# Moving a power and its followers by two steps on GpSimd, and joining eight group sums into five, in a fused graph network kernel

## The chip, the cores and the metric

The kernel runs on one core of one Trainium2 chip. The metric is the device time of one execution in microseconds (us). Names of the engines in the profile: PE is TensorE (PEld its weight loads), DVE is VectorE, ACT is ScalarE, POOL is GpSimd, SP is SyncE, which here only issues DMAs.

## The reference

64 graphs with 128 nodes and 128 features, and a dense weighted adjacency each. A first part (five small graph convolutions over subsets of the first 25 nodes) is added to x and normalised; a second part (five layers of aggregation and a gated recurrent cell over all 128 nodes) is added to that and normalised again.

```python
GROUPS = [list(range(25)), list(range(9)), [0, 9, 10, 11, 12, 13, 14],
          [6, 7, 8, 12, 13, 14], [3, 4, 5, 9, 10, 11]]
def graph_conv(x, adj, W, b):
    A = adj + eye(n)
    deg = sum(A, -1)
    dinv = where(deg == 0, 0, deg ** -0.5)
    return relu((dinv[:, :, None] * A * dinv[:, None, :]) @ (x @ W) + b)
fused = 0
for g, idx in enumerate(GROUPS):
    h = graph_conv(x[:, idx], adj[:, idx][:, :, idx], W1[g], b1[g])
    fused[:, idx] += softmax(fusion_w)[g] * graph_conv(h, ..., W2[g], b2[g])
x = layernorm(x + fused)
h = x
for l in range(5):
    agg = (adj != 0)^T @ (h @ weight[l])
    r, z = sigmoid(...), sigmoid(...)      # of agg and h
    n = tanh(i_n + r * h_n)
    h = (1 - z) * n + z * h
x = layernorm(x + h * mask)
```

## The kernel before

**Work and steps.** The 64 graphs are 4 chunks of 16 (CHUNKS), a chunk is 4 visits of 4 graphs (SB). The recurrent part goes through 80 windows, here called steps: for each chunk 5 layers times 4 visits, so 20 steps make a round, numbered `w.i` from 0 to 19. Neighbouring steps are of different visits, so that the engines can overlap them. A step is, on TensorE, nine 512-column multiplications with the state's high and low part (lines 1063 to 1065 through `product`), transposes of an older state (`turn`, line 1050), nine multiplications with the aggregated neighbours, and the aggregation of a coming step (line 1057). On ScalarE it is the two sigmoids and the tanh (`ng`, line 622) and copies out of PSUM; on VectorE `cg` (884, 887), the end of the step before (`dg` times `zg`, 796, and the new state `hT`, 798), and the low parts `hlo` (784) and `glo` (790); on GpSimd the difference `dg = hT - ng` (434), which waits for the tanh.

**The first part rides along.** While chunk c is in its round, the first part of chunk c + 1 is spread over the steps of that round, at step numbers written out by hand in `Plan`. Each engine's program is one list in order, with semaphores between the engines; nothing is reordered at run time, so what stands ahead in an engine's list delays what is behind. For the place that concerns us, at step 7 and 8 TensorE and ScalarE make the results of the second convolution: `fused` (16 graphs in 32 columns each, group 0) and `part` (groups 1 to 4, line 514). At step 9 (GATHER) GpSimd adds the groups of `part` into `fused`. At step 10 (BACK) TensorE transposes `fused` back (line 1003, waiting for all ADDS sums), and VectorE adds that to `xn` (753) in steps 10, 12 and 13. From step 11 on VectorE takes the statistics (760, 764) and GpSimd turns them into `rs` and `nm` (394 to 399, with a power), with which ScalarE normalises (524).

**Two chunks ahead.** In rounds 0 and 1 the adjacency of chunk c + 2 is prepared as well: VectorE sums the degrees at step 8 (669 to 679), GpSimd raises them to the power -0.5 (337) behind the `dg` of step 8, VectorE multiplies the adjacency with them at the end of step 9 (`scaled`, 685 and 689), and GpSimd spreads the rows into block diagonal tiles (346, six instructions with 358) behind the `dg` of step 10. TensorE needs those at step 2 of the next round. Rounds 2 and 3 have none of this, and round 3 no next chunk at all.

**Opening.** The first part of chunk 0 runs ahead of the steps; there the sums of the groups are VectorE's (743), and GpSimd has the powers of chunks 0 and 1.

**The sums.** Groups 1 to 4 are lists of nodes; `runs` cuts a list into runs of neighbouring node numbers, 8 over the five tiles of groups 1 to 4 (72, 72, 16, 96 and four times 48 elements in each partition). Each sum waits for the one before it.

Of the kernel before, what the change touches and what calls it, by code (L numbers as in the profile page):

```python
# [5 lines left out]
GROUPS = [list(range(25)), [0, 1, 2, 3, 4, 5, 6, 7, 8], [0, 9, 10, 11, 12, 13, 14],  # L6
          [6, 7, 8, 12, 13, 14], [3, 4, 5, 9, 10, 11]]
NG = len(GROUPS)
FN = 25
NP = 32  # L10
# [7 lines left out]
CB = 16  # L18
CHUNKS = B // CB
# [7 lines left out]
TILES = [(0, 4, b) for b in range(0, CB, 4)] + [(1, 8, 0), (1, 8, 8)] + [(g, 16, 0) for g in (2, 3, 4)]  # L27
# [3 lines left out]
TB = [t for t in range(NT) if TILES[t][0] != 0]  # L31
OFF = {}
# [8 lines left out]
def runs(nodes):  # L41

    out = []
    for i, v in enumerate(nodes):
        if out and v == out[-1][1] + out[-1][2]:
            out[-1][2] += 1
        else:
            out.append([i, v, 1])
    return [tuple(r) for r in out]
# [29 lines left out]
class Plan:  # L79

    ADJ, Y, HA, HB, SA, SB, OA, OB, GATHER, BACK, REST = 2, 3, 4, 5, 6, 7, 7, 8, 9, 10, (12, 13)
    DEGREES, SCALED, SPREAD = 8, 9, 10
    ONES = {2: 0, 5: 1, 11: 2, 13: 3}
    STATS1 = {11: 0, 14: 1, 15: 2, 16: 3}
    APPLY1 = {12: [(0, 0)], 13: [(0, 1)], 15: [(1, 0)], 16: [(1, 1), (2, 0)], 17: [(2, 1), (3, 0)], 18: [(3, 1)]}
# [8 lines left out]
def next_chunk(w):  # L94

    return w.sg + 1 if w.sg + 1 < CHUNKS else None


def stats1(w):
    c = next_chunk(w)  # L100
    return None if c is None or w.i not in Plan.STATS1 else c * SLOTS + Plan.STATS1[w.i]
# [7 lines left out]
def stats2(w):  # L109
    return None if w.sg == 0 or w.i not in Plan.STATS2 else (w.sg - 1) * SLOTS + Plan.STATS2[w.i]  # L110
# [9 lines left out]
def build(nc, x, adj, nodemask, W1, b1, W2, b2, fusion_w, weight, w_ih, w_hh, b_ih, b_hh, out):  # L120
    f32, f32r = mybir.dt.float32, mybir.dt.float32r
    ALU, ACT, AX = mybir.AluOpType, mybir.ActivationFunctionType, mybir.AxisListType
    ctx = ExitStack()
    with ctx:
        ctx.enter_context(nc.allow_non_contiguous_dma(reason="small rows of the adjacency"))

        def sb(name, shape, dt=f32):
            return ctx.enter_context(nc.sbuf_tensor(name, shape, dt))
# [53 lines left out]
        fused = sb("fused", [128, CB * NP])  # L182
        part = sb("part", [128, COLS_B])
# [24 lines left out]
        def b1c(g, c):  # L208
# [22 lines left out]
        gathered, dev1, dev2, ln1_dve, ln1_pool, hT_ok = map(sem, (  # L231
            "gathered", "dev1", "dev2", "ln1_dve", "ln1_pool", "hT_ok"))
# [25 lines left out]
        def group_cols(g):  # L258

            mine = [t for t in TB if TILES[t][0] == g]  # L260
            return OFF[mine[0]], OFF[mine[-1]] + ROWS[mine[-1]]

        def n_runs(tiles):

            return sum(len(runs(GROUPS[TILES[t][0]])) for t in tiles)
        ADDS = n_runs(TB)
        SP_ADJ, ACT_ADJ, POOL_ADJ = TB[0:2] + TB[3:4] + TA[0:1], TB[2:3] + TB[4:5] + TA[1:2], TA[2:4]
        XT_SP, XT_POOL = range(0, NT - 2), range(NT - 2, NT)

        def gather_part(t, i, v, n):  # L270

            g, k, b0 = TILES[t]
            into = fused[:].rearrange("p (b n) -> p b n", n=NP)[:, b0:b0 + k, v:v + n]
            return into, part[:, OFF[t] + i * k:OFF[t] + (i + n) * k].rearrange("p (n k) -> p k n", k=k)

        @block.sync
        def _(sp):
# [43 lines left out]
        def _(pool):  # L321
# [12 lines left out]
            def power(c):  # L334

                pool.wait_ge(deg_ok, c + 1)
                nc.gpsimd.tensor_tensor(dinv[:, c, :], deg[:], minus_half[:], ALU.pow).then_inc(pow_ok, 1)
# [25 lines left out]
            def ones(visit):  # L363

                pool.wait_ge(xa_in, 64 * (visit // SLOTS) + 64)
                ab = an[:, visit * SB:(visit + 1) * SB, :]
                nc.gpsimd.tensor_scalar(ab, ab, 0.0, 0.0, ALU.is_equal, ALU.is_equal).then_inc(a_ok, 1)

            def gather(c):

                n_add = 0
                pool.wait_ge(oa_ok, c + 1)
                for t in TB:
                    g, k, b0 = TILES[t]
                    pool.wait_ge(ob_ok, (NG - 1) * c + g)
                    for i, v, n in runs(GROUPS[g]):
                        if n_add:
                            pool.wait_ge(gathered, ADDS * c + n_add)
                        n_add += 1
                        into, these = gather_part(t, i, v, n)  # L380
                        nc.gpsimd.tensor_tensor(into, into, these, ALU.add).then_inc(gathered, 1)  # L381

            def norm1(visit):

# [16 lines left out]
            def deviation1(visit):  # L401

                pool.wait_ge(ln1_st, visit + 1)
                o = visit % SLOTS
                deviation(ag1[:, o], rs1[:, o], nm1[:, o], dev1, visit).then_inc(ln1_rs, 1)

            def deviation2(visit):

                pool.wait_ge(ln2_st, visit + 1)
                o = visit % SLOTS  # L410
                deviation(ag2[:, o], rs2[:, o], nm2[:, o], dev2, visit).then_inc(ln2_rs, 1)
# [17 lines left out]
            for w in ALL_WINDOWS:  # L429
                c = next_chunk(w)  # L430
                if c is not None and w.i == Plan.GATHER:
                    gather(c)
                pool.wait_ge(n_ok, w.k + 1)
                nc.gpsimd.tensor_tensor(dg[:, w.k % 2, :], hT[:, w.slot, :], ng[:, w.k % 2, :], ALU.subtract).then_inc(d_ok, 1)  # L434
                if stats1(w) is not None:
                    deviation1(stats1(w))
                if stats2(w) is not None:
                    deviation2(stats2(w))
                if c is not None and w.i in Plan.ONES:
                    ones(c * SLOTS + Plan.ONES[w.i])  # L440
                if w.sg + 2 < CHUNKS and w.i == Plan.DEGREES:
                    power(w.sg + 2)
                if w.sg + 2 < CHUNKS and w.i == Plan.SPREAD:
                    spread(w.sg + 2)
# [193 lines left out]
        def _(dve):  # L638
            link = counter(dve, dve_c)
            TT, TS, STT = nc.vector.tensor_tensor, nc.vector.tensor_scalar, nc.vector.scalar_tensor_tensor  # L640
# [4 lines left out]
            for t, (g, k, _) in enumerate(TILES):  # L645
                for i, v, n in runs(GROUPS[g]):
                    nc.vector.memset(member[:, t, v:v + n], 1.0)
                    nc.vector.reduce_sum(unit[:, t, v:v + n],
                                         ident[:, i * k:(i + n) * k].rearrange("p (n k) -> p n k", k=k), AX.X)
# [80 lines left out]

            def gather(c):

                n_add = 0
                dve.wait_ge(oa_ok, c + 1)
                for t in TB:
                    g, k, b0 = TILES[t]
                    dve.wait_ge(ob_ok, (NG - 1) * c + g)
                    for i, v, n in runs(GROUPS[g]):
                        if n_add:
                            dve.wait_ge(gathered, ADDS * c + n_add)  # L740
                        n_add += 1
                        into, these = gather_part(t, i, v, n)
                        TT(into, into, these, ALU.add).then_inc(gathered, 1)

            def add(c, first, some=range(PACK)):

# [108 lines left out]
            for w in ALL_WINDOWS:  # L855
                k, s, p = w.k, w.slot, w.k % 2
                c = next_chunk(w)
# [50 lines left out]
        def _(pe):  # L908
# [90 lines left out]
            def back(c):  # L999

                pe.wait_ge(gathered, ADDS * (c + 1))
                for t in range(CB // PACK):
# [189 lines left out]
```

## Time and profile before

| what | value |
|---|---|
| median of 3 runs | 559.54 us (559.19 to 559.57) |
| profiled execution | 555.05 us |
| its span, first to last instruction | 553.0 us |
| TensorE busy | 521.4 us, 94% |
| VectorE busy | 436.0 us, 79% |
| ScalarE busy | 369.4 us, 67% |
| GpSimd busy | 253.0 us, 46% |
| mean granted clock of TensorE | 0.983 of full |

A busy share is an average over the opening (the first 50 us), the rounds and the closing. The chain of work that ended last goes through TensorE for 67% of the span, VectorE for 11% and GpSimd for 8%. Starts of rows count from the start of the span. Ends of matrix multiplications are modelled, since they overlap each other; the distance from start to start tells the pace.

### The profile page before, as it was taken

Reading aid. Unit: us, or ns where it says so; the run is one execution under the profiler, and the core shown is the slowest. Engines: PE = TensorE matmul, PEld = TensorE weight load, DVE = VectorE, ACT = ScalarE, POOL = GpSimd, SP = SyncE. Lnnn points to the kernel's source line nnn. Section 1 sums busy time; section 2 is a strip of 40 time slices with the busy share of each in tenths; the row PEclk is TensorE's granted clock in tenths of the full one; section 3 lists DMA queues with packets and bytes.
Section 4 is the critical chain, followed back from the end, with each engine's and each line's share of the span. In section 5 each row is a group of like instructions: output and inputs, shape, how many; then the busy total and the mean of one; then the engine's idle time right before and its main releaser. Section 6 shows DMA issues by size and latency. Waiting matters only on the chain.

```text
span 553.0 us, 8593 instructions
## 1 busy us (share of the span) xinstructions
PE 521.4 (94%) x3021; PEld 446.0 (81%) x3021; DVE 436.0 (79%) x970; ACT 369.4 (67%) x682; POOL 253.0 (46%) x304
## 2 busy tenths in 40 slices
PE   8886999989999999989999999999999999999980
PEld 7775888868888889868888888888888888888860
DVE  4276765779988986879988986779988998878785
ACT  2434765656785766777787667677887678886644
POOL 7167333267543245376552344364552335432335
PEclk9898999999999999999999999999999999999995
DMA  4966610000000000000000000000000000010002
GB/s 103 247 177 162 159 33 3 1 0 1 2 1 1 0 28 25 21 20 21 0 2 1 0 1 21 20 20 20 0 1 1 2 1 20 22 36 0 2 1 76
DMA packets 35666, 17.30 MB, mean 31 GB/s; under 512 B 4429, under 2 KB 35584, under 8 KB 35624
## 3 DMA queue, kind: packets, MB, share of 16 engines
q1 hardware_dynamic: 32569, 15.13, 10.4%
q10 hardware_dynamic: 2639, 1.42, 0.9%
q8 instruction: 25, 0.41, 0.3%
q0 software_dynamic: 416, 0.20, 0.2%
q14 instruction: 17, 0.14, 0.1%
HBM read 12.54 MB, written 4.19 MB: 30 GB/s over the span
## 4 chain that ended last, share of the span: by engine, by line
PE 67%; DVE 11%; POOL 8%; ACT 5%; issue 4%; SPq 2%; DMA 1%; DVEq 0%; POOLq 0%; ACTq 0%
PE p L1065 15%; PE p L1063 15%; PE p L1064 14%; PE p L1057 9%; PE p L1050 6%; POOL dg L434 3%; PE p L958 3%; POOL fused L381 2%; DVE cg L884 2%; DVE cg L887 2%; PE p L932 2%; POOL rs L397 1%; DVE xn L753 1%; PE p L951 1%; PE p L941 1%
## 5 line engine op out<-in xcount | busy, mean ns | idle before, releaser
L434 POOL TENSOR_TENSOR dg<-hT,ng 128x512 f32<-128x512 f32 x80 | 124.9, 1561 | 262.4 <-ACT ng L622 262.4
L1063 PE MATMUL p<-hhi,wh 128*128 128x512 f32 x240 | 101.1, 421 | 0.6 <-DVE hlo L784 0.6
L1063 PE MATMUL p<-ghi,wf 128*128 128x512 f32 x240 | 101.7, 424 | 0.0
L1065 PE MATMUL p<-ghi,wf 128*128 128x512 f32 x240 | 94.8, 395 | 0.0
L1065 PE MATMUL p<-hhi,wh 128*128 128x512 f32 x240 | 94.3, 393 | 0.0
L1064 PE MATMUL p<-glo,wf 128*128 128x512 f32 x240 | 94.1, 392 | 0.0
L1064 PE MATMUL p<-hlo,wh 128*128 128x512 f32 x240 | 93.7, 390 | 0.0
L884 DVE SCALAR_TENSOR_TENSOR cg<-p,biasc,rg 128x512 f32<-128x512 f32 x80 | 59.9, 748 | 41.1 <-ACT rg L609 40.4
L609 ACT ACTIVATE rg<-p,gb 128x512 f32<-128x512 f32 x80 | 55.4, 692 | 36.5 <-PE p L1065 31.0
L622 ACT ACTIVATE ng<-cg,biasc 128x512 f32<-128x512 f32 x80 | 57.9, 723 | 24.0 <-DVE cg L887 23.8
L1057 PEld LDWEIGHTS p<-an,nat 128*128 128x128 f32 x512 | 66.9, 191 | 5.2
L620 ACT ACTIVATE zg<-p,gb 128x512 f32<-128x512 f32 x80 | 55.0, 688 | 19.5 <-PE p L1065 19.5
L1057 PE MATMUL p<-an,nat 128*128 128x128 f32 x512 | 67.4, 275 | 0.0
L784 DVE TENSOR_TENSOR hlo<-hT,hhi 128x512 fp32r<-128x512 f32 x76 | 66.5, 876 | 0.9
L887 DVE TENSOR_TENSOR cg<-cg,p 128x512 f32<-128x512 f32 x80 | 55.0, 688 | 8.7 <-DVE cg L884 0.5
L790 DVE TENSOR_TENSOR glo<-p,ghi 128x512 fp32r<-128x512 f32 x80 | 55.2, 690 | 7.6 <-ACT ghi L578 7.6
L798 DVE TENSOR_TENSOR hT<-ng,dg 128x512 f32<-128x512 f32 x80 | 55.5, 694 | 2.8
L607 ACT COPY nat<-p 128x512 f32<-128x512 f32 x64 | 37.8, 591 | 27.1 <-PE p L1050 26.5
L796 DVE TENSOR_TENSOR dg<-zg,dg 128x512 f32<-128x512 f32 x80 | 55.5, 694 | 0.0
L1050 PE MATMUL p<-ident,hT 128*128 128x128 f32 x320 | 49.0, 276 | 6.9 <-DVE hT L798 6.6
L1065 PEld LDWEIGHTS p<-ghi,wf 128*128 128x128 f32 x240 | 45.3, 189 | 10.5
L1065 PEld LDWEIGHTS p<-hhi,wh 128*128 128x128 f32 x240 | 45.0, 188 | 10.0
(131 smaller groups left out, 853.1 us busy)
## 6 DMA issues: line engine op xcount, KB each, us to landing
xn<-in_x_dram SPq DMA_DIRECT2D x8, 512.0 KB, 4.8
an<-in_adj_dram SPq DMA_DIRECT2D x8, 512.0 KB, 7.1
out_dram<-xn SPq DMA_DIRECT2D x16, 256.0 KB, 2.3
xt<-in_x_dram SPq DMA_DIRECT2D x16, 50.0 KB
w<-in_L_gnn_W_dram ACTq DMA_DIRECT2D x1, 640.0 KB, 6.9
w<-in_L_gnn_W_dram SPq DMA_DIRECT2D x1, 640.0 KB, 7.9
zg<-in_L_gnn_weight_dram ACTq DMA_DIRECT2D x1, 320.0 KB, 7.9
xt<-in_x_dram SPq DMA_DIRECT2D x8, 36.0 KB
```

The lines of the kernel that those rows point to most:

```text
L434: nc.gpsimd.tensor_tensor(dg[:, w.k % 2, :], hT[:, w.slot, :], ng[:, w.k % 2, :], ALU.subtract).then_inc(d_ok, 1)
L622: nc.scalar.activation(ng[:, p, :], cg[:, p, :], ACT.Tanh, bias=bin_).then_inc(n_ok, 1)
L784: TT(hlo[:, m % SLOTS, :], hT[:, m % SLOTS, :] if source is None else source[:], hhi[:, m % SLOTS, :], ALU.subtract).then_inc(lo_ok, 1)
L796: TT(dg[:, p, :], zg[:, p, :], dg[:, p, :], ALU.mult).then_inc(e_ok, 1)
L798: TT(hT[:, s, :], ng[:, p, :], dg[:, p, :], ALU.add).then_inc(h_ok, 1)
L884: STT(cg[:, p, :], PH[:], bhn, rg[:, p, :], ALU.add, ALU.mult).then_inc(t1_ok, 1)
L887: TT(cg[:, p, :], cg[:, p, :], PI[:], ALU.add).then_inc(c_ok, 1)
L1050: last = TR(bank[:, q * 128:(q + 1) * 128], src(q), ident[:])
L1057: last = MM(bank[:, q * N:(q + 1) * N], src(q), an[:, b + q, :], start=True, stop=True)
L1063: MM(bank[:], w[:, 0, cols], xhi, start=start, stop=False)
L1064: MM(bank[:], w[:, 0, cols], xlo, start=False, stop=False)
L1065: return MM(bank[:], w[:, 1, cols], xhi, start=False, stop=stop)
```

## The change

GpSimd's power of the degrees is moved from step 8 to step 10 (still behind `dg`), VectorE's scaling from the end of step 9 to the end of step 11, GpSimd's spreading from step 10 to step 12. VectorE's summing of the degrees stays in step 8. The eight sums of the groups become five, on GpSimd in the rounds and on VectorE in the opening: one for both tiles of group 1 (144 elements), two for group 2 (96 and 16), one each for groups 3 and 4 (96), whose two runs of three nodes lie six apart and are put into one access pattern. A sum waits for an earlier one only where both write the same nodes.

```diff
--- before.py
+++ after.py
@@ -79,7 +79,7 @@
 class Plan:
 
     ADJ, Y, HA, HB, SA, SB, OA, OB, GATHER, BACK, REST = 2, 3, 4, 5, 6, 7, 7, 8, 9, 10, (12, 13)
-    DEGREES, SCALED, SPREAD = 8, 9, 10
+    DEGREES, POWER, SCALED, SPREAD = 8, 10, 11, 12
     ONES = {2: 0, 5: 1, 11: 2, 13: 3}
     STATS1 = {11: 0, 14: 1, 15: 2, 16: 3}
     APPLY1 = {12: [(0, 0)], 13: [(0, 1)], 15: [(1, 0)], 16: [(1, 1), (2, 0)], 17: [(2, 1), (3, 0)], 18: [(3, 1)]}
@@ -263,15 +263,25 @@
         def n_runs(tiles):
 
             return sum(len(runs(GROUPS[TILES[t][0]])) for t in tiles)
-        ADDS = n_runs(TB)
         SP_ADJ, ACT_ADJ, POOL_ADJ = TB[0:2] + TB[3:4] + TA[0:1], TB[2:3] + TB[4:5] + TA[1:2], TA[2:4]
         XT_SP, XT_POOL = range(0, NT - 2), range(NT - 2, NT)
 
-        def gather_part(t, i, v, n):
-
-            g, k, b0 = TILES[t]
-            into = fused[:].rearrange("p (b n) -> p b n", n=NP)[:, b0:b0 + k, v:v + n]
-            return into, part[:, OFF[t] + i * k:OFF[t] + (i + n) * k].rearrange("p (n k) -> p k n", k=k)
+        def gather_parts():
+
+            rows_ = fused[:].rearrange("p (b n) -> p b n", n=NP)
+
+            def cols(g):
+                a, b = group_cols(g)
+                return part[:, a:b]
+            yield 1, 0, (rows_[:, :, 0:9].rearrange("p (t k) n -> p t k n", t=2),
+                         cols(1).rearrange("p (t n k) -> p t k n", t=2, n=9))
+            yield 2, 0, (rows_[:, :, 9:15], cols(2)[:, CB:].rearrange("p (n k) -> p k n", k=CB))
+            yield 2, 1, (rows_[:, :, 0:1], cols(2)[:, 0:CB].rearrange("p (n k) -> p k n", k=CB))
+            for g in (3, 4):
+                v = GROUPS[g][0]
+                yield g, 2, (rows_[:, :, v:v + 12].rearrange("p k (s n) -> p s n k", s=2)[:, :, 0:3, :],
+                             cols(g).rearrange("p (s n k) -> p s n k", s=2, n=3))
+        ADDS = 5
 
         @block.sync
         def _(sp):
@@ -368,17 +378,12 @@
 
             def gather(c):
 
-                n_add = 0
                 pool.wait_ge(oa_ok, c + 1)
-                for t in TB:
-                    g, k, b0 = TILES[t]
+                for g, done, (into, these) in gather_parts():
                     pool.wait_ge(ob_ok, (NG - 1) * c + g)
-                    for i, v, n in runs(GROUPS[g]):
-                        if n_add:
-                            pool.wait_ge(gathered, ADDS * c + n_add)
-                        n_add += 1
-                        into, these = gather_part(t, i, v, n)
-                        nc.gpsimd.tensor_tensor(into, into, these, ALU.add).then_inc(gathered, 1)
+                    if done:
+                        pool.wait_ge(gathered, ADDS * c + done)
+                    nc.gpsimd.tensor_tensor(into, into, these, ALU.add).then_inc(gathered, 1)
 
             def norm1(visit):
 
@@ -438,7 +443,7 @@
                     deviation2(stats2(w))
                 if c is not None and w.i in Plan.ONES:
                     ones(c * SLOTS + Plan.ONES[w.i])
-                if w.sg + 2 < CHUNKS and w.i == Plan.DEGREES:
+                if w.sg + 2 < CHUNKS and w.i == Plan.POWER:
                     power(w.sg + 2)
                 if w.sg + 2 < CHUNKS and w.i == Plan.SPREAD:
                     spread(w.sg + 2)
@@ -730,17 +735,12 @@
 
             def gather(c):
 
-                n_add = 0
                 dve.wait_ge(oa_ok, c + 1)
-                for t in TB:
-                    g, k, b0 = TILES[t]
+                for g, done, (into, these) in gather_parts():
                     dve.wait_ge(ob_ok, (NG - 1) * c + g)
-                    for i, v, n in runs(GROUPS[g]):
-                        if n_add:
-                            dve.wait_ge(gathered, ADDS * c + n_add)
-                        n_add += 1
-                        into, these = gather_part(t, i, v, n)
-                        TT(into, into, these, ALU.add).then_inc(gathered, 1)
+                    if done:
+                        dve.wait_ge(gathered, ADDS * c + done)
+                    TT(into, into, these, ALU.add).then_inc(gathered, 1)
 
             def add(c, first, some=range(PACK)):
 
```

## Rows read from the trace of the kernel before

**Rows 1.** Busy times of the engines on the page: us, share of the span, instructions.

```profile
PE 521.4 (94%) x3021; PEld 446.0 (81%) x3021; DVE 436.0 (79%) x970; ACT 369.4 (67%) x682; POOL 253.0 (46%) x304
```

**Rows 2.** Timeline of TensorE: start, duration, instruction, [idle before].

```profile
119.17 0.39 PE L1064 MATMUL p<-hlo,wh 128*128 128x512 f32 x1
119.40 0.39 PE L1065 MATMUL p<-hhi,wh 128*128 128x512 f32 x1
121.79 0.66 PE L1003 MATMUL p<-ident,fused 128*128 128x128 f32 x4 [2.00 <-POOL fused L381]
...
138.89 0.60 PE L1050 MATMUL p<-ident,hT 128*128 128x128 f32 x4
...
248.16 0.65 PE L1003 MATMUL p<-ident,fused 128*128 128x128 f32 x4 [2.05 <-POOL fused L381]
...
371.99 0.39 PE L1065 MATMUL p<-hhi,wh 128*128 128x512 f32 x1
372.45 0.66 PE L1003 MATMUL p<-ident,fused 128*128 128x128 f32 x4
```

**Rows 3.** Timeline of GpSimd (POOL), steps 8 to 13 of round 0.

```profile
115.18 2.28 POOL L337 TENSOR_TENSOR dinv<-deg,minus_half 128x9 f32<-128x9 f32 x1
117.42 4.32 POOL L381 TENSOR_TENSOR fused<-fused,part 128x72 f32<-128x72 f32 x8
...
128.40 0.84 POOL L346 TENSOR_TENSOR bda<-am,ksel 100x400 f32<-100x400 f32 x1
129.21 1.98 POOL L358 TENSOR_TENSOR bdb<-am,ksel 72x144 f32<-72x144 f32 x5
132.19 1.64 POOL L434 TENSOR_TENSOR dg<-hT,ng 128x512 f32<-128x512 f32 x1 [1.00 <-ACT ng L622]
133.92 1.08 POOL L394 TENSOR_SCALAR rs<-ag 128x4 f32<-128x4 f32 x1
...
138.74 1.29 POOL L434 TENSOR_TENSOR dg<-hT,ng 128x512 f32<-128x512 f32 x1 [0.29 <-ACT ng L622]
144.03 1.63 POOL L434 TENSOR_TENSOR dg<-hT,ng 128x512 f32<-128x512 f32 x1 [4.00 <-ACT ng L622]
```

**Rows 4.** Chain that ended last, sums of round 2: start, duration, what.

```profile
367.80 0.81 POOL fused L381
```

**Rows 5.** Timelines of the opening, of TensorE, VectorE (DVE) and GpSimd.

```profile
30.84 3.42 PE L913 MATMUL p<-ng,cg 128*128 128x384 f32 x10
34.62 0.66 PE L1003 MATMUL p<-ident,fused 128*128 128x128 f32 x4 [0.36 <-DVE fused L743]
...
31.61 2.95 DVE L743 TENSOR_TENSOR fused<-fused,part 128x72 f32<-128x72 f32 x8 [0.37 <-ACT part L514]
...
31.24 1.84 POOL L337 TENSOR_TENSOR dinv<-deg,minus_half 128x9 f32<-128x9 f32 x1 [0.96 <-DVE deg L678]
```

**Rows 6.** Timeline of VectorE, steps 9 to 13 of round 0.

```profile
119.87 0.40 DVE L689 TENSOR_TENSOR am<-am,dinv 128x225 f32<-128x225 f32 x1
...
129.02 0.77 DVE L784 TENSOR_TENSOR hlo<-hT,hhi 128x512 fp32r<-128x512 f32 x1
...
135.31 0.75 DVE L884 SCALAR_TENSOR_TENSOR cg<-p,biasc,rg 128x512 f32<-128x512 f32 x1 [0.37 <-ACT rg L609]
...
137.70 0.69 DVE L798 TENSOR_TENSOR hT<-ng,dg 128x512 f32<-128x512 f32 x1
139.15 0.69 DVE L790 TENSOR_TENSOR glo<-p,ghi 128x512 fp32r<-128x512 f32 x1 [0.76 <-ACT ghi L578]
...
140.94 0.67 DVE L784 TENSOR_TENSOR hlo<-hT,hhi 128x512 fp32r<-128x512 f32 x1
```

**Rows 7.** Timelines of GpSimd and VectorE beside a power, step 14 of round 0.

```profile
151.37 1.04 POOL L397 TENSOR_TENSOR rs<-rs,minus_half 128x4 f32<-128x4 f32 x1
...
151.43 0.67 DVE L784 TENSOR_TENSOR hlo<-hT,hhi 128x512 fp32r<-128x512 f32 x1
```

**Rows 8.** Timeline of ScalarE (ACT), step 12 of round 0.

```profile
136.58 0.89 ACT L524 ACTIVATE xn<-xn,nm,rs 128x128 f32<-128x128 f32 x2 [1.30 <-POOL nm L399]
```

## Prediction

> **What bounds the kernel now.** I read four things in this order. First the page's busy line: TensorE is busy 94% of the span, so outside the opening and the closing every pause of TensorE should count in full [rows 1]. Second, TensorE's own timeline, looking for the places where it pauses. Its 512-column multiplications normally start 0.23 us apart (119.17, 119.40). In step 9 to 10 of a round that rhythm breaks ahead of the four transposes of line 1003, which turn the group sums back. In the first round (round 0) the last multiplication starts at 119.40, so the transposes could start at 119.63, and they start at 121.79: a pause of 2.16 us. The row of 121.79 itself gives 2.00, counted from the modelled end, and that of the second round 2.05, so the second pause is 2.16 + 0.05 = 2.21 us. In the third (round 2) the start is due at 371.99 + 0.23 = 372.22 and comes at 372.45: only 0.23 us [rows 2]. Third, GpSimd's timeline at that place, to see what is late. In the first round GpSimd does the power of the degrees (2.28 us), then eight sums in 4.32 us, and they end at 121.74, which releases the transposes [rows 3]. The third round has no chunk two ahead of it, so it has no power there; its eight sums start right behind dg. That round is an experiment that the kernel already holds: without the power the pause is 0.23 us. Fourth, VectorE: behind the transposes it adds the result to x and goes on with a chain that has hardly a pause for several steps, so a later start of the transposes is not won back.
>
> **Part 1, the power leaves the path.** In rounds 0 and 1 (the only ones with a chunk two ahead) the power stood at the end of step 8, directly ahead of the sums. With it gone the sums start at 115.2 instead of 117.42. Even at their old length of 4.32 us they would end at 119.5 to 119.8: what is left is the 0.23 us of round 2. So this part alone gives 2.16 - 0.23 = 1.93 and 2.21 - 0.23 = 1.98 us, together 3.9 us.
>
> **Part 2, five sums for eight.** The number of elements is the same (448 per partition); three instructions go, and most waits of one on the one before. The eight old ones take 4.32 us, 0.54 each with the gaps [rows 3]; the dearest, 72 elements with VectorE in the way, is 0.81 [rows 4]. No row shows 144 elements, nor these two patterns over four dimensions. From below: five at 0.54 are 2.7 us; from above: five at the dearest 0.81 are 4.05 us. I take 3.1, nearer the lower end, since the time goes with the instructions more than with the elements, but the average one is now larger. TensorE's room is 119.63 - 115.2 = 4.4 us, so even the upper bound meets it, and TensorE itself then sets the start. That removes the last 0.23 us in each of the three rounds: 0.7 us. The rest of the shortening is hidden behind TensorE's step 10.
>
> **Part 3, the sums of chunk 0 on VectorE.** They take 2.95 us from 31.61 to 34.56. TensorE is at its weight products from 30.84 to 34.26 and starts the transposes at 34.62 [rows 5]. However short the sums become, the transposes can't start before 34.26: the gain is at most 0.36 us and I take 0.35. They wait for the same four group results of ScalarE as the old ones, whose last group began its sums before 34.3 too; for the new ones to be late, five would have to take 2.65 of the 2.95 us that eight took. What follows (addition to x, statistics, the deviation on GpSimd, normalising on ScalarE) is a chain that keeps its length.
>
> Sum of the gains: 2.16 + 2.21 + 0.23 + 0.35 = 4.95, say 5.0 us.
>
> **Part 4, where the power goes.** In step 10 it now stands behind dg, at 128.4, where the spreading was. The spreading took 0.84 + 1.98 = 2.8 us there, and dg of step 11 came at 132.19 after a pause of 1.00 us [rows 3]. The power takes 2.3 us, so dg of step 11 is not late and the pause merely grows. Cost nothing for GpSimd. It is covered by ScalarE's tanh, for which dg waits; without that cover it would be 2.3 us a round.
>
> What it does to VectorE: VectorE's hlo at 129.02 falls in it [rows 6]. Some VectorE operations with both inputs in SBUF do stand still beside GpSimd. A power does not seem to do that: at 151.37 GpSimd starts a power of 1.04 us, and hlo starts at 151.43 and takes 0.67 us, its usual time [rows 7]; in the opening the eight sums on VectorE begin during the power of 31.24 to 33.08 [rows 5]. I take nothing. The Trainium skill says otherwise ("SBUF — State Buffer", § on the shared port pair): a VectorE operation with two SBUF inputs and a GpSimd operation that reads SBUF exclude each other for the whole instruction. By that rule hlo would wait for the end of the power, which is a rival below; by the rows the sum stays as it is.
>
> **Part 5, where the scaling goes.** Its larger instruction is that of 119.87 with 0.40 us; the smaller, on 9 elements, stands ahead of it and I put it and the gap at a third of the whole, so 0.6 us together. They cost nothing in step 9, since VectorE waited behind them for the late transposes [rows 6]. Now they stand at the end of step 11, at about 133.2. VectorE has a pause of 0.37 us at 135.31, so 0.2 us is left, or up to 0.8 if the first of them waits for dg of step 11, which runs until 133.83 (132.19 + 1.64). VectorE meets ScalarE again at 139.15, after a pause of 0.76 us, and that takes up nearly all. But hT of 137.70 ends at 138.39, and TensorE reads it at 138.89 with 0.5 us to spare [rows 2, 6]: 0 to 0.3 us reach TensorE. There is a second way to it: the deviation behind dg. Its first instruction took 1.08 us at 133.92, plainly held by VectorE, and ScalarE stood 1.30 us for its result at 136.58 [rows 3, 8]. With VectorE 0.6 us longer without a gap, this may end 0.6 to 1.1 us later, or earlier, if the scaling opens a gap in which it slips through. I take 0.2 us a round for the scaling; bounds 0 and 1.1.
>
> **Part 6, where the spreading goes.** It stands behind dg of step 12, from 140.03 on (dg of 138.74 takes 1.29), in the pause of 4.00 us before the next dg at 144.03 [rows 3], so its 2.8 us fit. VectorE's hlo at 140.94 and the two ends of the step after it are on the path here. Beside the spreading, hlo of 129.02 took 0.77 instead of 0.67 [rows 6]: 0.1 us. I take 0.2 us a round; bounds 0 and 0.66 (one whole spreading instruction in the way, a third of 1.98). The next user of its result is TensorE in step 2 of the next round, far off, as is that of the power.
>
> **Sum.** 5.0 - 2 x (0.2 + 0.2) = 4.2 us. The durations are those of one profiled execution of 555.05 us (span 553.0 and 2.05 around it); it would become 550.9. The median of the runs, 559.54, is 4.5 us above that execution, and nothing says that the steps differ, so I carry the difference over: 559.54 - 4.2 = 555.3 us.
>
> **The rivals.**
> (A) The power holds VectorE. The power of 1.84 us (its length in the opening) would run from 128.4 to 130.25, and hlo end at 130.92 instead of 129.79: 1.1 us in a chain without pauses, twice, 2.2 us on top. Time: 557.5. This is what the skill's page on SBUF would make of it. Against it stand rows 5 and 7; for it, that hlo does lose time beside other GpSimd work.
> (B) The scaling holds the deviation of step 11 and the spreading hits hlo: 1.1 + 0.66 a round instead of 0.4, gain 5.0 - 3.5 = 1.5 us. Time: 558.0, or 557 with half of it. For it: the 1.08 us and ScalarE's 1.30 us of waiting. Against: ScalarE and VectorE meet again at 139.15 with 0.76 us of slack on VectorE.
> (C) The opening's gain is lost on its way, in a wait of the first steps for something else; gain 0.35 less. Time 555.6, inside the forecast.
> (D) The other side, slower: the two patterns over four dimensions are dear on GpSimd. It decides from the point at which five sums exceed 4.4 us in every round (0.88 each); to be slower by 0.2% the power's whole gain must go too, so five must take over 7 us in rounds 0 and 1 and in round 2, above 1.4 us each, and the time would then be 561. dg with 512 elements takes 1.29 to 1.64 us [rows 3], so 96 elements at 1.4 would cost what five times as many cost there.
> (E) The change does not do what it says: the sums still start late, since something other than the power held them. Round 2 speaks against it: without a power they start at once. Time 559.5.
>
> **How the numbers follow.** The forecast, gain 3.2 to 5.2 us with the small costs at 0 to 0.9 a round, has 0.72 and its own range is 554.3 to 556.4. A has 0.09, B 0.12, D 0.03, E 0.04. 0.2% is 1.1 us, about what a measurement of this kernel can tell. A and B still end faster, most of the time: faster 0.90, same 0.07, slower 0.03. The range must leave out no more than 2 in 10: from 554.1 (all costs at nothing is 554.5, less 0.4 for the spread of the runs) to 557.8, which takes in A and most of B.
>
> **What the changed profile would show.** Right: TensorE's pause before line 1003 under 0.1 us in all three rounds; the sums ending at 118 to 119 on the old scale; a power of 1.8 to 2.3 us in step 10 and hlo beside it at 0.67; line 1003 in the opening 0.35 us earlier. Wrong: hlo of step 11 above 1.3 us (A); the deviation of step 11 ending over 0.5 us later behind dg, or hlo of step 13 at 1.2 (B); one sum over 0.9 us (D). A round between the same steps in rounds 0 and 1 should be 1.8 us shorter, that of round 2 0.2.

## The result and the profile after

| | kernel before | changed kernel |
|---|---|---|
| first comparison, median of 5 runs | 559.19 us (555.90 to 559.57) | 551.67 us (551.22 to 552.77) |
| ratio and 95% interval | | 0.9892 (0.9864 to 0.9920) |
| second comparison, medians of 10 and 6 runs | 557.73 us (556.09 to 559.12) | 551.84 us (549.44 to 553.24) |
| ratio and 95% interval | | 0.9891 (0.9869 to 0.9913) |
| profiled execution | 555.05 us, span 553.0 | 552.77 us, span 550.6 |

The change is faster by 1.1%, some 6 us. The recorded forecast, 555.3 us in a range from 554.1 to 557.8, gave it 4.2 us. The medians of one comparison lie 7.5 us apart and the two profiled spans 2.4, so the question is not only where the change gained, but also what moves the kernel before, unchanged, between 555 and 561 us.

To separate the two, the executions are cut at instructions that both kernels have: the first product of line 932 of chunks 1, 2 and 3 (in step 3 of rounds 0, 1 and 2), and the last transposes of the state.

| stretch, us | before | changed | gain |
|---|---|---|---|
| start to chunk 1's product (the opening) | 70.09 | 72.91 | -2.82 |
| to chunk 2's product | 126.31 | 123.84 | 2.47 |
| to chunk 3's product | 126.27 | 123.79 | 2.48 |
| to the last transposes of the state (the last way) | 220.52 | 220.23 | 0.29 |
| rest | 9.83 | 9.82 | 0.01 |

The rounds give 5.24 us. The opening of this execution was slower, and most of that comes ahead of any changed instruction: the weight products start at 33.41 us instead of 30.84, 2.57 us later. From 15 to 25 us TensorE's granted clock was 0.56 and 0.50 of full in two stretches of 5 us, and 0.87 and 0.79 in the kernel before; 1.00 is 2.4 GHz and 0.50 is 1.2 GHz. The way from the transposes of chunk 0 to chunk 1's product is 0.78 us longer too, with a clock of 0.50 from 51 to 56 us where the kernel before had 0.82 (more below). The page's busy line and the shares of its chain by engine [rows 1]:

```profile
PE 523.7 (95%) x3021; PEld 449.4 (82%) x3021; DVE 435.0 (79%) x967; ACT 370.3 (67%) x682; POOL 248.9 (45%) x295
...
PE 86%; DVE 5%; ACT 2%; SPq 2%; POOL 2%; DMA 1%; issue 1%; ACTq 0%; POOLq 0%; DVEq 0%
```

TensorE now carries 86% of the chain that ended last, where it had 67%. Its timeline around the transposes, with the multiplication ahead of them, answers to [rows 2]:

```profile
122.22 0.40 PE L1065 MATMUL p<-hhi,wh 128*128 128x512 f32 x1
122.45 0.60 PE L1003 MATMUL p<-ident,fused 128*128 128x128 f32 x4
...
139.47 0.66 PE L1050 MATMUL p<-ident,hT 128*128 128x128 f32 x4
...
246.07 0.40 PE L1065 MATMUL p<-hhi,wh 128*128 128x512 f32 x1
246.30 0.60 PE L1003 MATMUL p<-ident,fused 128*128 128x128 f32 x4
...
369.85 0.40 PE L1065 MATMUL p<-hhi,wh 128*128 128x512 f32 x1
370.09 0.60 PE L1003 MATMUL p<-ident,fused 128*128 128x128 f32 x4
```

All three start 0.23 or 0.24 us behind the last multiplication, which is the normal pace. The pauses of 2.16, 2.21 and 0.23 us are gone. GpSimd in steps 8 to 13 of round 0, as in [rows 3]:

```profile
116.40 1.64 POOL L439 TENSOR_TENSOR dg<-hT,ng 128x512 f32<-128x512 f32 x1 [5.37 <-ACT ng L627]
117.99 2.47 POOL L386 TENSOR_TENSOR fused<-fused,part 128x144 f32<-128x144 f32 x5
...
128.99 1.83 POOL L347 TENSOR_TENSOR dinv<-deg,minus_half 128x9 f32<-128x9 f32 x1
132.78 1.65 POOL L439 TENSOR_TENSOR dg<-hT,ng 128x512 f32<-128x512 f32 x1 [1.97 <-ACT ng L627]
134.51 0.42 POOL L399 TENSOR_SCALAR rs<-ag 128x4 f32<-128x4 f32 x1
...
138.93 1.64 POOL L439 TENSOR_TENSOR dg<-hT,ng 128x512 f32<-128x512 f32 x1 [0.45 <-ACT ng L627]
140.53 0.85 POOL L356 TENSOR_TENSOR bda<-am,ksel 100x400 f32<-100x400 f32 x1
141.34 1.98 POOL L368 TENSOR_TENSOR bdb<-am,ksel 72x144 f32<-72x144 f32 x5
```

The five sums take 2.47 us and end at 120.46, 2.0 us before TensorE wants them. The power has 1.83 us and not the 2.28 of its old place. VectorE in steps 11 to 13 [rows 6], with hlo, the two instructions of the scaling (690 and 694), the addition to x (753), and the hlo of step 13:

```profile
129.61 0.66 DVE L784 TENSOR_TENSOR hlo<-hT,hhi 128x512 fp32r<-128x512 f32 x1
...
133.82 0.63 DVE L690 TENSOR_TENSOR dinv<-dinv,zero 128x9 f32<-128x9 f32 x1
134.49 0.40 DVE L694 TENSOR_TENSOR am<-am,dinv 128x225 f32<-128x225 f32 x1
134.79 1.11 DVE L753 TENSOR_TENSOR xn<-xn,p 25x384 f32<-25x384 f32 x2
...
141.14 0.79 DVE L784 TENSOR_TENSOR hlo<-hT,hhi 128x512 fp32r<-128x512 f32 x1
```

hlo at 129.61 runs through the power of 128.99 to 130.82 in 0.66 us. The scaling's first instruction takes 0.63 us instead of 0.15 and ends with dg (132.78 + 1.65 = 134.43). And behind dg GpSimd's first instruction of the deviation, at 134.51, takes 0.42 us, where it took 1.08. In the kernel before VectorE was doing this beside it:

```profile
133.23 1.11 DVE L753 TENSOR_TENSOR xn<-xn,p 25x384 f32<-25x384 f32 x2
134.27 0.67 DVE L784 TENSOR_TENSOR hlo<-hT,hhi 128x512 fp32r<-128x512 f32 x1
```

There the deviation's instruction started at 133.92, beside the addition, and ended at 135.00, 0.06 us behind hlo (134.94). Now it starts beside the scaling's larger instruction and ends at 134.93, 0.04 us behind that one (134.89), while the addition and hlo are still to come. ScalarE, which normalises with the deviation's result, waits 0.73 us instead of 1.30 [rows 8]:

```profile
136.61 0.88 ACT L529 ACTIVATE xn<-xn,nm,rs 128x128 f32<-128x128 f32 x2 [0.73 <-POOL nm L404]
```

The opening [rows 5], TensorE and VectorE: the sums of chunk 0 take 1.31 instead of 2.95 us, and the transposes start 3.25 us behind the first weight product instead of 3.78.

```profile
33.41 3.42 PE L913 MATMUL p<-ng,cg 128*128 128x384 f32 x10
36.66 0.60 PE L1003 MATMUL p<-ident,fused 128*128 128x128 f32 x4
...
34.18 1.31 DVE L743 TENSOR_TENSOR fused<-fused,part 128x144 f32<-128x144 f32 x5 [0.37 <-ACT part L519]
```

### The profile page after: what moved, and what is told of

Its sections match the earlier page's. It is cut to its first block, busy times and chain, and to the rows that moved or that the text cites. A ratio compares the mean times of both kernels' runs of the same rounds, so it can differ in the third digit from the quotient of the medians.

```text
span 550.6 us, 8577 instructions
## 1 busy us (share of the span) xinstructions
PE 523.7 (95%) x3021; PEld 449.4 (82%) x3021; DVE 435.0 (79%) x967; ACT 370.3 (67%) x682; POOL 248.9 (45%) x295
## 3 DMA queue, kind: packets, MB, share of 16 engines
q10 hardware_dynamic: 2639, 1.42, 0.9%
## 4 chain that ended last, share of the span: by engine, by line
PE 86%; DVE 5%; ACT 2%; SPq 2%; POOL 2%; DMA 1%; issue 1%; ACTq 0%; POOLq 0%; DVEq 0%
PE p L1065 19%; PE p L1063 19%; PE p L1064 19%; PE p L1057 12%; PE p L1050 8%; PE p L958 3%; PE p L932 2%; PE p L951 1%; PE p L941 1%; DMA xt<-in_x_dram 1%; SPq L250 1%; PE p L996 1%; SPq L245 1%; POOL rs L402 1%; DVE cg L884 1%
## 5 line engine op out<-in xcount | busy, mean ns | idle before, releaser
L1050 PEld LDWEIGHTS p<-ident,hT 128*128 128x128 f32 x320 | 38.5, 142 | 17.9 <-DVE hT L798 11.3
```

The costliest lines, as they stand in the source:

```text
L1050: last = TR(bank[:, q * 128:(q + 1) * 128], src(q), ident[:])
```

## The experiments

**Unchanged (0).** The kernel before against itself.

> The kernel before, unchanged, timed against itself. Theory 1 (the part of the result that the rounds of steps do not explain is a chance state of TensorE's clock in the opening): ratio 1.000, single runs spread over 555 to 560 us, the slower ones with a lower mean granted clock. Theory 2 (the kernel before has a fixed slower opening which the change mends): ratio 1.000 too, but the runs lie within 1 us of each other at 559 and the profiled 555 was an exception.

Measured: 558.17 us (555.93 to 559.63, 12 runs) against 557.76 (555.02 to 560.80, 29 runs), ratio 1.0001 (0.9980 to 1.0022). Both theories had the ratio at 1.000; the spread of the runs is theory 1's. One kernel spreads over 5.8 us, and the spread goes with the clock: the run of 555.02 has a mean granted clock of 0.983, those of 560.80 and 560.56 have 0.970. The 555.05 us of the kernel's own profiled execution were at the short end. The one profiled here took 559.31. Most of the difference lies in the opening (72.99 us to chunk 1's product here, 70.09 before), but not all: round 0 took 127.87 us instead of 126.31. The stretches before and behind its pause say why (length, then busy us of PE, PEld, DVE, ACT and POOL, then the granted clock, DMA share and GB/s):

```profile
122.00:124.60 2.60, 0.69 (x4) 0.23 (x2) 1.14 (x4) 0.62 (x1) 2.08 (x6) 1.00 0.00 0
124.60:126.60 2.00, 1.90 (x9) 1.90 (x10) 0.80 (x3) 0.08 (x1) 1.27 (x2) 0.59 0.00 0
126.60:128.60 2.00, 2.00 (x6) 1.52 (x6) 1.00 (x4) 1.20 (x2) 0.00 (x0) 0.56 0.00 0
128.60:131.00 2.40, 2.40 (x16) 2.12 (x15) 2.26 (x4) 1.48 (x3) 0.10 (x1) 1.00 0.02 7
```

The timeline of TensorE there:

```profile
124.70 0.93 PE L1003 MATMUL p<-ident,fused 128*128 128x128 f32 x4 [2.01 <-POOL fused L381]
...
127.14 0.63 PE L1065 MATMUL p<-ghi,wf 128*128 128x512 f32 x1
127.56 0.63 PE L1063 MATMUL p<-ghi,wf 128*128 128x512 f32 x1
...
128.40 0.39 PE L1065 MATMUL p<-ghi,wf 128*128 128x512 f32 x1
128.63 0.40 PE L1063 MATMUL p<-ghi,wf 128*128 128x512 f32 x1
```

After the pause of 2.01 us ahead of the transposes the granted clock fell from 1.00 to a mean of 0.59 and 0.56 in the next two stretches, each partly at 2.4 GHz and mostly at 1.2; multiplications started 0.42 us apart instead of 0.23 (127.14, 127.56), and at 128.40 the pace was back. I read this as a second price of the pause, 1.6 us when it comes; that the pause is the cause is inferred from the order in time. It came in one of the eight long pauses that four profiled executions with the old order show (this one, the kernel before, experiments 3 and 8), and in none of the thirteen profiled executions did the clock fall anywhere else between opening and closing.

**Only the move (1).** The eight sums stay.

```diff
-    DEGREES, SCALED, SPREAD = 8, 9, 10
+    DEGREES, POWER, SCALED, SPREAD = 8, 10, 11, 12
...
-                if w.sg + 2 < CHUNKS and w.i == Plan.DEGREES:
+                if w.sg + 2 < CHUNKS and w.i == Plan.POWER:
```

> Only the power, the scaling and the spreading are moved; the eight sums stay. Theory 1: the pause ahead of the transposes falls to 0.23 us in each of the three chunks (gain 1.93 + 1.98), and the scaling in step 11 lets the deviation of that step through on GpSimd (0.25 us in each of rounds 0 and 1): 4.4 us shorter than before at equal opening. By the recorded prediction (scaling and spreading cost 0.4 a round): 3.1 us. The deviation's first instruction in step 11 takes 0.4 and not 1.1 us in rounds 0 and 1, by theory 1.

Measured: 552.72 us (6 runs), ratio 0.9907 (0.9874 to 0.9939). Rounds 0 and 1 take 124.17 us each, the last way 220.65: gains of 2.14 + 2.10 - 0.13 = 4.1 us at equal opening, near the 4.4 of theory 1. The medians are 5.0 us apart, and the interval of the ratio reaches from 3.4 to 7.0 us. TensorE's transposes and GpSimd's sums and deviation:

```profile
122.03 0.66 PE L1003 MATMUL p<-ident,fused 128*128 128x128 f32 x4
...
117.32 4.65 POOL L381 TENSOR_TENSOR fused<-fused,part 128x72 f32<-128x72 f32 x8
...
134.15 0.42 POOL L394 TENSOR_SCALAR rs<-ag 128x4 f32<-128x4 f32 x1
```

The move takes the pause down to what round 2 had, and the deviation has its 0.42 us.

**Only the five sums (2).** The power stays in step 8, the scaling in 9, the spreading in 10.

```diff
-    DEGREES, POWER, SCALED, SPREAD = 8, 10, 11, 12
+    DEGREES, POWER, SCALED, SPREAD = 8, 8, 9, 10
```

> Only the five sums, on GpSimd and in the opening on VectorE; the power stays ahead of them in step 8. The sums took 2.47 us instead of 4.32 in the changed kernel. Theory 1: they end 1.85 us earlier, the pause ahead of the transposes is 0.3 to 0.4 us in rounds 0 and 1 and none in round 2: gain 1.8 + 1.8 + 0.25 + 0.5 in the opening = 4.4 us, nearly what the move gives alone, so that the two together give far less than their sum. Rival: the sums are held by VectorE at this place and save only 1 us each: gain 2.8.

Measured: 553.86 us (12 runs), ratio 0.9931 (0.9907 to 0.9956). Rounds 125.31 and 125.25, last way 220.24, and 0.5 us in the opening: 1.00 + 1.02 + 0.28 + 0.5 = 2.8 us at equal opening. Theory 1 had 4.4 and was wrong by the rounds; the rival's number is met, and in part for the rival's reason. TensorE, GpSimd and VectorE in step 9:

```profile
121.29 0.66 PE L1003 MATMUL p<-ident,fused 128*128 128x128 f32 x4 [0.58 <-POOL fused L386]
...
118.34 2.89 POOL L386 TENSOR_TENSOR fused<-fused,part 128x144 f32<-128x144 f32 x5
121.18 1.28 POOL L439 TENSOR_TENSOR dg<-hT,ng 128x512 f32<-128x512 f32 x1
...
121.29 1.42 DVE L694 TENSOR_TENSOR am<-am,dinv 128x225 f32<-128x225 f32 x1
```

The sums take 2.89 us here and not the 2.47 of the changed kernel. Two-input operations of VectorE lie beside them, and are longer too (that of line 796 takes 0.88 us instead of 0.69). So the sums end 1.4 us earlier instead of 1.85, and the pause is 0.58 us. Then dg of step 9 follows at 121.18 and meets the scaling on VectorE: its larger instruction takes 1.42 us instead of 0.40. With the difference of the openings (71.01 to 70.09 us) taken off, the addition to x behind it starts 0.85 us earlier than before, not 1.4. By step 13 TensorE has kept 1.0 of the 1.4 us. In the changed kernel, with power and scaling moved, neither loss is seen: 2.47 us for the sums and 0.40 for the scaling's larger instruction.

**Only the opening's sums (3).** VectorE adds chunk 0 in five instructions, GpSimd the others in eight.

```diff
-        ADDS = n_runs(TB)
+        def added(c):
+            return 0 if c == 0 else 5 + n_runs(TB) * (c - 1)
...
-                pe.wait_ge(gathered, ADDS * (c + 1))
+                pe.wait_ge(gathered, added(c + 1))
```

> Only the sums of chunk 0, in the opening, are five; everything else is as before. Theory 1: 0.5 us shorter, and the same spread of openings as the kernel before, so a ratio of 0.998 to 1.000. Theory 2 (the earlier transposes change TensorE's clock in the opening for good): 2 us or more shorter and a higher mean granted clock in all runs.

Measured: 556.33 us (554.57 to 559.58, 12 runs), ratio 0.9981 (0.9957 to 1.0005). From the weight products to the transposes it is 3.25 us instead of 3.78, the rounds are as before (126.30, 126.25). Theory 1: half a microsecond, and the openings spread as before.

**The scaling later (5).** The changed kernel with the scaling in step 13 and the spreading in step 14.

```diff
-    DEGREES, POWER, SCALED, SPREAD = 8, 10, 11, 12
+    DEGREES, POWER, SCALED, SPREAD = 8, 10, 13, 14
```

> The changed kernel with the scaling in step 13 instead of 11 and the spreading in step 14 instead of 12. Theory 1 (in step 11 the scaling's two short instructions on VectorE open a gap in which the deviation's first instruction gets through on GpSimd, and that is worth 0.2 us a round): the first instruction of the deviation takes 1.08 us again, ScalarE waits 1.3 us for it in step 12, and rounds 0 and 1 are 0.2 us longer than the changed kernel's 123.8 us between the same instructions. Theory 2 (the 0.2 us came from the spreading leaving step 10, and the scaling is free): rounds 0 and 1 stay at 123.8 us or get shorter.

Measured: 556.26 us in a single run; rounds 0 and 1 take 126.66 and 126.62 us, 2.8 more than the changed kernel's. VectorE's scaling in step 13, GpSimd's deviation of step 11, and TensorE's pauses in steps 15 and 17:

```profile
143.55 0.63 DVE L690 TENSOR_TENSOR dinv<-dinv,zero 128x9 f32<-128x9 f32 x1
144.21 0.77 DVE L694 TENSOR_TENSOR am<-am,dinv 128x225 f32<-128x225 f32 x1
...
132.43 1.08 POOL L399 TENSOR_SCALAR rs<-ag 128x4 f32<-128x4 f32 x1
...
149.59 0.66 PE L1050 MATMUL p<-ident,hT 128*128 128x128 f32 x4 [0.47 <-DVE hT L798]
...
161.23 0.50 PE L1063 MATMUL p<-hhi,wh 128*128 128x512 f32 x1 [1.00 <-ACT zg L625]
```

The first half is as theory 1 had it: with the scaling gone from step 11 the deviation takes 1.08 us, and the steps there last 5.62 and 5.67 us, from one group of transposes of line 1050 to the next (131.77, 137.39, 143.06), as before the change (5.64 and 5.68, from 133.25, 138.89 and 144.57), although the spreading is out of step 10. In the changed kernel they last 5.63 and 5.51 (133.84, 139.47, 144.98). So the 0.2 us belong to the scaling. The size of the rest was not foreseen: in step 13 the same two instructions stand in a chain of VectorE without any pause, and TensorE's steps grow to 6.53 and later, with the spreading in step 14, to 6.80 us. How the 2.8 us divide between the two is not separated by any run.

**Work added in round 2 (6).** Two VectorE instructions like the scaling's, on tiles no longer used.

```diff
+                if w.sg == 2 and w.i == Plan.SCALED:
...
+                    TT(deg[:], zero[:], zero[:], ALU.add).then_inc(prep_c, 1)
+                    dve.wait_ge(prep_c, 6 * CHUNKS + 1)
+                    TT(am[:].rearrange("p t m -> p (t m)"), unit[:].rearrange("p t m -> p (t m)"),
+                       member[:].rearrange("p t m -> p (t m)"), ALU.mult).then_inc(prep_c, 1)
```

> The changed kernel with work added: in round 2, which has no scaling, two VectorE instructions of the same sizes as the scaling's, on tiles no longer used, stand at the end of step 11. Theory 1: the deviation's first instruction in round 2 takes 0.4 instead of 1.08 us, and the way from the first product of step 3 of round 2 to the last transposes of the state (220.23 us) gets 0.2 us shorter, although VectorE has 0.55 us more to do. Theory 2 (VectorE's extra work is a cost, hidden or not): that way is as long or up to 0.4 us longer.

Measured: the last way takes 220.02 instead of 220.23 us; the single run took 548.91 us. The deviation's first instruction in round 2, on GpSimd:

```profile
378.59 0.42 POOL L399 TENSOR_SCALAR rs<-ag 128x4 f32<-128x4 f32 x1
```

More work on VectorE, 0.21 us less on the last way, as theory 1 said. Here too the instruction starts beside the larger of the two added ones and ends 0.05 us behind it (378.96). The 548.91 us themselves say nothing: the opening of this execution was 3.6 us shorter than that of the changed kernel's.

**The opening held warm (7 and 8).** Idle transposes where TensorE waits, in the changed kernel (7) and in the kernel before (8); nothing uses what they write.

```diff
+            stay_warm(14, P[2])
             neighbours(0)
...
                 if k == 0:
+                    stay_warm(34, PT)
                     pe.wait_ge(prep_lo, 6)
```

> The changed kernel with idle transposes on TensorE where it waits in the opening: 14 ahead of the first products of chunk 0 and 34 in step 0 ahead of the transposes of visit 1. Their results are used by nothing. Theory 1 (the spread of the runs and 2 to 5 us of their time is TensorE's clock at its lower level in the opening, behind these two waits): the runs lie within 1 us of each other, 3 us or more below the changed kernel's 551.7, mean granted clock 0.99. Rival: the clock falls whatever TensorE does there: same time and spread.

> The kernel before with the same idle transposes in the opening. With the opening held steady the difference of this kernel to the changed one with the same transposes is the change's own effect. Theory 1: 2.47 + 2.48 + 0.29 us in the rounds and 0.5 in the opening, 5.7 us. Recorded prediction: 4.2 us. Rival (the change also mends the clock of the opening): both kernels with idle transposes are less than 5 us apart.

Measured: 546.57 us (546.22 to 547.03, 4 runs), ratio to the kernel before 0.9797 (0.9772 to 0.9822), for the changed kernel; 552.06 us (551.62 to 555.02, 6 runs), ratio 0.9907 (0.9879 to 0.9936), for the other. The two are 5.5 us apart, and the profiled executions agree: 2.39 + 2.49 + 0.37 = 5.25 us in the rounds and the last way, and 0.5 between weight products and transposes. The whole openings of these two executions are equal (67.21 and 67.19 us), since in experiment 7 the weight products started 0.56 us later; why is open. The granted clock (third number from the end) in the opening of experiment 7, in two stretches:

```profile
12.00:30.00 18.00, 15.71 (x129) 14.41 (x129) 7.15 (x24) 8.34 (x21) 5.18 (x10) 1.00 0.87 227
45.00:58.00 13.00, 12.44 (x84) 11.06 (x83) 8.00 (x26) 8.30 (x15) 11.43 (x26) 1.00 0.64 153
```

and in the opening of the changed kernel's profiled execution:

```profile
12.00:30.00 18.00, 15.17 (x86) 12.99 (x85) 5.37 (x19) 7.44 (x20) 5.65 (x10) 0.72 0.87 230
49.00:58.00 9.00, 6.49 (x28) 5.64 (x29) 4.17 (x18) 4.92 (x10) 8.21 (x20) 0.62 0.44 96
```

It went from 0.72 and 0.62 to 1.00 in both, and chunk 1's product from 72.91 to 67.21 us. The spread is less clear. Experiment 7's four runs lie 0.8 us apart, as expected; the changed kernel's lay 1.6 apart in the first comparison and 3.8 in experiment 11 (549.44 to 553.24). But experiment 9, with the same opening, spreads over 1.9 us, and experiment 8 over 3.4. The slowest run of experiment 8 (555.02, clock 0.982) would fit the clock falling in a long pause of the rounds, but it was not the profiled one; and one run of experiment 9, without such pauses, has 547.82 us at a clock of 0.983. So more than the long pauses moves the time, and what it is stays open.

**Warm, with the added work (9), and warm, with hlo first (10).** Both have the idle transposes of experiment 7. Experiment 9 adds the two instructions of experiment 6, experiment 10 changes VectorE's order in step 12:

```diff
-                    if w.i in Plan.REST:
-                        add(c, False, range(2) if w.i == Plan.REST[0] else range(2, PACK))
+                    if w.i == Plan.REST[1]:
+                        add(c, False, range(2, PACK))
...
                     lo_state(k + 2)
+                if c is not None and w.i == Plan.REST[0]:
+                    add(c, False, range(2))
```

> The changed kernel with the idle transposes of the opening and the two added VectorE instructions in step 11 of round 2. Theory 1: the deviation's first instruction takes 0.4 us in all three rounds, the last way is 220.0 us, and the time is 0.2 us below the 546.6 of the kernel with the transposes alone: 546.4.

> The changed kernel with the idle transposes of the opening, and in step 12 VectorE makes the low part of the state ahead of its addition to x instead of behind it. Theory 1 (the operation with two SBUF inputs that queues on VectorE behind the addition keeps the deviation's first instruction waiting): with that operation directly behind dg, the deviation starts as soon as it is over, so its first instruction takes 0.4 to 0.7 us and not 1.08 in round 2, and the last way is 0.1 to 0.2 us shorter than 220.23. Theory 2 (the addition itself holds the deviation): still 1.08 us or more, since now the two additions follow.

Measured: 546.77 us (545.88 to 547.82, 5 runs) with a last way of 220.03, for experiment 9, whose deviation has its 0.42 us in round 2 too (its median was expected 0.2 us below experiment 7's and is 0.2 above, within the spread), and 546.19 us (545.72 to 546.57, 4 runs), ratio 0.9794 (0.9777 to 0.9810), with a last way of 219.76, for experiment 10. Experiment 10 in round 2, VectorE and GpSimd:

```profile
375.04 1.00 DVE L784 TENSOR_TENSOR hlo<-hT,hhi 128x512 fp32r<-128x512 f32 x1
375.97 1.11 DVE L753 TENSOR_TENSOR xn<-xn,p 25x384 f32<-25x384 f32 x2
...
375.58 0.52 POOL L399 TENSOR_SCALAR rs<-ag 128x4 f32<-128x4 f32 x1
376.18 0.19 POOL L400 TENSOR_SCALAR nm<-ag 128x4 f32<-128x4 f32 x1
```

hlo now waits for dg (1.00 us) and ends at 376.04; the deviation's instruction, stuck since 375.58, ends at 376.10 and runs beside the additions that follow. So it is the operation with two SBUF inputs that holds it, not the addition with one input in PSUM. An addition that is already under way doesn't hold GpSimd either: the deviation's next instruction starts within the first of the two and takes its usual 0.2 us.

The last way is 0.47 us shorter, more than the 0.1 to 0.2 expected. Rounds 0 and 1 stay at 123.8 us. Of all the versions this is the fastest, though 9 and 10 are no measurable step beyond 7.

**The changed kernel again (11).**

> The changed kernel once more. Theory 1 (5.2 us from the rounds, 0.5 from the opening, the rest of the first comparison chance of the opening): 5.7 us below the kernel before, ratio 0.9898, single runs spread over 2 to 5 us with their clock. Rival (the first comparison's 7.5 us between medians is the true effect): 0.9866.

Measured: 551.84 against 557.73 us, ratio 0.9891, as in the table above. Its rounds are 123.81 and 123.82, its last way 220.23.

## Why the prediction was wrong

**Right.** The place and the cause: the pauses of 2.16, 2.21 and 0.23 us ahead of the transposes were the gain, and they fell to nothing. The power costs nothing in step 10: hlo beside it took 0.66 us, so rival A did not come true. The sums are not the bound (2.47 us, less than the 2.7 of the lower end). Part 2 had the time go more with the instructions than with the elements. In the traces both count: one sum takes 0.22 us for 16 elements, 0.44 for 96 and 0.60 for 144 (experiment 2). But 1.0 of the 1.85 us saved are the gaps between the instructions, 0.08 to 0.15 us each among the eight old sums, which wait for each other, and none among the five. The shorter sums of chunk 0 give what TensorE's weight products allow, 0.53 us where 0.35 was taken: the start was due 3.25 us behind them, not at their modelled end of 3.42.

**Wrong, first step: parts 5 and 6.** They charged the scaling and the spreading with 0.4 us a round, so that a round should have become 1.8 us shorter; it became 2.47. What was measured is a gain of 0.25 a round beside the pause (2.47 - 2.22, the step from 114.12 to 122.29, now from 116.94 to 122.89, having become 2.22 us shorter). The prediction named the way, "or earlier, if the scaling opens a gap in which it slips through", and priced it at nothing. The sign is as in that clause, but it is not a gap that lets the instruction in: the two instructions of the scaling are 0.04 us apart, and the deviation's first instruction starts when the second of them is under way. In the old order it came beside the addition, with hlo queued next on VectorE, and was kept from 133.92 until the end of hlo. Now it comes beside the scaling's larger instruction and is kept only until the end of that one, ahead of the addition and of hlo. Experiments 1, 5 and 6 show it with and without the two instructions; no run has them without the semaphore wait between them. The spreading in step 12 made hlo 0.12 us longer (0.79 at 141.14), and TensorE did not feel it: 5.51 us for that step instead of 5.68. In all 2 x (0.4 + 0.25) = 1.3 us of the miss.

**Wrong, second step: the carrying over to the median.** The step "nothing says that the steps differ, so I carry the difference over" took a median of three runs, 559.54, for the time of the kernel before. 29 runs give 557.76. So the reference itself was 1.8 us too high, and the range allowed 0.4 for it. What the 4.5 us between the profiled execution and that median were, experiment 0 shows at a like time (559.31): 2.9 us in the opening and 1.6 behind the pause of round 0, both with TensorE's clock at its lower level. The runs behind the median itself have no trace. With the change's own 5.8 us (5.24 in the rounds, 0.53 in the opening) on 557.76, 552.0 comes out, and 551.7 and 551.8 were measured.

The two steps make 3.1 of the 3.6 us by which the forecast missed, and 0.2 more are the opening.

**Left out altogether:** that a pause of 2 us can cost more than its length. In experiment 0 the clock was down behind it, for 1.6 us more. How often that happens is open: one pause in eight is too few for a rate, and the 0.1 to 0.3 us between 5.8 and the measured differences of medians is within their uncertainty.

## What to carry to other kernels

Look for a round that lacks one part of the work: the pauses of rounds 0, 1 and 2 side by side gave the main term within 0.1 us, ahead of any run. A move has to be read on two engines that share operands: the same two short instructions took 1.8 instead of 0.6 us beside dg, gained 0.2 in step 11, where they put off the hlo that held GpSimd before, and in step 13, with the spreading behind them in step 14, made a round 2.8 us longer. And before a time is compared, know what spreads it: here idle transposes in two waits of the opening took 5 us off the changed kernel's time, and the 13 runs with them (experiments 7, 9 and 10) lie within 2.1 us, where the 11 without lie within 3.8.

## What the runs showed of the hardware

GpSimd and VectorE exclude each other by the kind of operation. VectorE's operations with two SBUF inputs wait for dg: the scaling's small instruction 0.63 instead of 0.15 us, hlo 1.00 instead of 0.66, the scaling's larger one 1.42 instead of 0.40. An instruction of GpSimd waits for such an operation too, and ends 0.04 to 0.06 us behind it: 0.42, 0.52 or 1.08 instead of 0.20 us. In the 1.08 us it came 0.35 us ahead of hlo's own start (133.92 and 134.27), while the addition ran. An addition alone does not hold it (experiment 10), so I take it that hlo, queued next, held it already; no run tests that by itself. The Trainium skill ("SBUF — State Buffer", § Who interferes with whom) pairs two SBUF inputs against a GpSimd operation that reads SBUF, and lets whoever issues first go first. The trace agrees on the pairing; on who goes first it agrees where one of the two is under way, but not by the starts of the 1.08 us. The Trainium skill also says that the pair is held for the whole instruction, and that does not hold for the power: hlo ran in 0.66 us within a power of 1.83 us, and within the 1.04 us of [rows 7] too.

TensorE's clock fell in the opening, from 1.00 (2.4 GHz) to 0.50 (1.2 GHz) in whole stretches of 5 us: in the changed kernel from 20 to 25 us, behind waits of 1.23 and 1.43 us (ahead of 13.44 and 16.98), and from 51 to 56, around a wait of 4.27 us (ahead of 51.51). Once it fell behind a pause of 2.01 us in the middle of a dense stretch, and seven like pauses had no such fall. With idle transposes in two of the opening's waits it stayed at 1.00.
